# Expert loops of a macaron block: one buffer of gathered rows per tile, all gathers issued ahead of the scatters

## What is computed

```python
x = x + 0.5 * ffn(layernorm(x))     # mixture of 8 experts, top 1
x = x + mamba(layernorm(x))         # selective scan, 16 states
x = x + 0.5 * ffn(layernorm(x))     # same experts again

def ffn(x):
    route = softmax(x @ router_w + router_b)      # 8 experts
    max_prob, max_ind = max(route), argmax(route)
    for e in range(8):
        a, g = split(x @ w1[e])                   # 128 -> 2 x 512
        y = silu(a) * g @ w2[e]                   # 512 -> 128
        out = where(max_ind == e, y, out)
    return out * max_prob
```

## Time and profile before

| | |
|---|---|
| median of 3 runs | 427.21 us |
| span of the profiled execution | 449.5 us |
| TensorE matmul busy | 394.2 us, 88% |
| VectorE busy | 320.5 us, 71% |
| ScalarE busy | 264.8 us, 59% |
| GpSimd busy | 257.3 us, 57% |
| mean granted TensorE clock | 0.943 of full |

### The profile page before, as it was taken

How to read it: one execution, slowest core, us unless ns; L and a number is a source line. 1 busy time by engine, 2 the same in 40 slices (tenths; PEclk the granted TensorE clock), 3 DMA queues, 4 the chain that set the end, 5 groups by cost and what they waited for, 6 DMA issues and landing times. The chain is left out here.

```text
span 449.5 us, 8650 instructions
## 1 busy us (share of the span) xinstructions
PE 394.2 (88%) x3052; PEld 359.0 (80%) x3052; DVE 320.5 (71%) x497; ACT 264.8 (59%) x488; POOL 257.3 (57%) x186
## 2 busy tenths in 40 slices
PE   7978889994998899999998999998838886997894
PEld 7967889994763478899988899997838886997894
DVE  3664545552897999999999999999485853554452
ACT  3214333440597999999999999993443123342340
POOL 5045657543001049999999999998400063566633
PEclk9699999998799999999999999999965798999998
DMA  7828491111200484435344443441450311111200
GB/s 210 277 71 245 120 400 50 37 33 50 72 1 6 124 61 107 142 125 164 123 152 142 129 162 121 156 139 49 169 206 0 98 35 33 34 40 43 45 29 25
DMA packets 42731, 47.48 MB, mean 106 GB/s; under 512 B 13313, under 2 KB 34370, under 8 KB 42178
## 3 DMA queue, kind: packets, MB, share of 16 engines
q1 hardware_dynamic: 39746, 40.80, 30.1%
q0 software_dynamic: 2944, 6.13, 5.5%
HBM read 37.38 MB, written 9.54 MB: 104 GB/s over the span
## 5 line engine op out<-in xcount | busy, mean ns | idle before, releaser
L858 POOL TENSOR_TENSOR w_sb<-phase,w_sb 128x1024 f32<-128x1024 f32 x62 | 144.7, 2371 | 0.0
L939 DVE TENSOR_TENSOR_SCAN phase<-phase,psum 128x1024 f32<-128x1024 f32 x64 | 142.1, 2271 | 3.1 <-PE psum L1080 2.3
L648 PE MATMUL psum<-phase 128*128 128x128 f32 x736 | 91.4, 278 | 0.1
L376 POOL DMA_INDIRECT phase<-token_rows,token_row x46 | 46.9, 1020 | 76.4 <-DVE token_row L481 63.0
L648 PEld LDWEIGHTS psum<-phase 128*128 128x128 f32 x736 | 87.3, 194 | 0.4 <-issue 0.4
L996 ACT ACTIVATE phase<-dtxT,B_cols 128x256 f32<-128x256 f32 x192 | 80.2, 507 | 0.3
L1098 PE MATMUL psum<-ident,w_sb 128*128 128x128 f32 x512 | 67.8, 276 | 4.7 <-POOL w_sb L858 1.4
L1006 ACT ACTIVATE phase<-dt,neg_A 128x1024 f32<-128x1024 f32 x64 | 70.0, 1147 | 0.0
L1098 PEld LDWEIGHTS psum<-ident,w_sb 128*128 128x128 f32 x512 | 56.3, 141 | 10.6 <-POOL w_sb L858 8.9
L502 DVE TENSOR_TENSOR phase<-phase,psum 128x512 f32<-128x512 f32 x46 | 31.5, 685 | 45.9 <-PE psum L648 20.2
L563 ACT ACTIVATE phase<-psum 128x512 f32<-128x512 f32 x46 | 27.4, 595 | 60.2 <-PE psum L648 44.2
(11 more groups left out here) (171 smaller groups left out, 421.7 us busy)
## 6 DMA issues: line engine op xcount, KB each, us to landing
w_sb<-c_rows SPq DMA_DIRECT2D x32, 512.0 KB, 3.8
w_sb<-ffn_w SPq DMA_DIRECT2D x16, 512.0 KB, 7.2
B_diag<-dt SPq DMA_DIRECT2D x4, 1024.0 KB
phase<-B_diag SPq DMA_DIRECT2D x32, 128.0 KB, 3.7
token_rows<-x_tok SPq DMA_DIRECT2D x8, 264.0 KB, 4.4
w_sb<-ffn_w SPq DMA_DIRECT2D x8, 256.0 KB, 7.8
x_tok<-attn_x SPq DMA_DIRECT2D x4, 256.0 KB, 4.3
x_tok<-x_rows SPq DMA_DIRECT2D x4, 256.0 KB, 3.9
```

The source lines that it names most:

```text
L376: nc.gpsimd.indirect_dma_start(xs_sb[:, t % XS_RING, :], None, token_rows, bass.IndirectOffsetOnAxis(ap=token_row[:, t:t + 1], axis=0)).th ...
L648: last = nc.tensor.matmul(psum[:, 2 * k + part, c * P:(c + 1) * P], w1_tile[:, t % W1_RING, part * F + c * P:part * F + (c + 1) * P], xsT_ ...
L858: nc.gpsimd.tensor_tensor(hC[:, k % HC_RING, :], H[:, k % H_RING, :], C_sb[:, j % C_RING, :], ALU.mult).then_inc(M["hC_ready"], 1)
L939: nc.vector.tensor_tensor_scan(H[:, k % H_RING, :], dA[:, k % DECAY_RING, :], dBx_bank[k % SLOTS], 0.0, ALU.mult, ALU.add).then_inc(M["sca ...
```

## The change

A buffer of gathered rows for every tile (23 in place of 10). GpSimd issues all 23 gathers of a layer one behind the other and then all 23 scatters. The ten semaphores of the gathers stay, so gather t from 10 on now waits until gather t - 10 has landed, in place of waiting for give(t - 10). The ring of four results stays.

```diff
-    XS_RING, AHEAD, YS_RING = 10, 8, 4
+    XS_SEMS, YS_RING = 10, 4
...
-            (P, XS_RING, RW), (P, TURN_RING, D), (P, TURN_RING, P), (P, W1_RING, 2 * F), (P, 2, F), (P, U_RING, F),
+            (P, SLOT_TILES, RW), (P, TURN_RING, D), (P, TURN_RING, P), (P, W1_RING, 2 * F), (P, 2, F), (P, U_RING, F),
...
+        def await_rows(engine, f, t):
+            engine.wait_ge(f["xs_loaded"][t % XS_SEMS], f["xs_before"][t % XS_SEMS] + 16 * (t // XS_SEMS + 1))
+
         def ffn_gpsimd(pool, f, into):
 
             def gather(t):
                 if t == FULL:
                     pool.wait_ge(f["token_row_ready"], 2)
-                if t >= XS_RING:
-                    pool.wait_ge(f["ys_ready"], t - XS_RING + 1)
-                nc.gpsimd.indirect_dma_start(xs_sb[:, t % XS_RING, :], None, token_rows,
+                if t >= XS_SEMS:
+                    await_rows(pool, f, t - XS_SEMS)
+                nc.gpsimd.indirect_dma_start(xs_sb[:, t, :], None, token_rows,
...
-            for t in range(AHEAD):
+            for t in range(SLOT_TILES):
                 gather(t)
             for t in range(SLOT_TILES):
-                if t + AHEAD < SLOT_TILES:
-                    gather(t + AHEAD)
                 scatter(t)
```

More of the change, by code:

```diff
@@ L224, in ffn_sems @@
         def ffn_sems(tag, n):
-            xs_before = [16 * n * len(range(k, SLOT_TILES, XS_RING)) for k in range(XS_RING)]
+            xs_before = [16 * n * len(range(k, SLOT_TILES, XS_SEMS)) for k in range(XS_SEMS)]
             f = {n: sem(f"{tag}_{n}") for n in (
@@ L235, in ffn_sems @@
             return f
-        xs_loaded = [sem(f"xs_loaded{k}") for k in range(XS_RING)]
+        xs_loaded = [sem(f"xs_loaded{k}") for k in range(XS_SEMS)]
         ys_stored = [sem(f"ys_stored{k}") for k in range(YS_RING)]
@@ L373, in gather @@
                     pool.wait_ge(f["token_row_ready"], 2)
-                if t >= XS_RING:
-                    pool.wait_ge(f["ys_ready"], t - XS_RING + 1)
-                nc.gpsimd.indirect_dma_start(xs_sb[:, t % XS_RING, :], None, token_rows,
+                if t >= XS_SEMS:
+                    await_rows(pool, f, t - XS_SEMS)
+                nc.gpsimd.indirect_dma_start(xs_sb[:, t, :], None, token_rows,
                                              bass.IndirectOffsetOnAxis(ap=token_row[:, t:t + 1], axis=0)
-                                             ).then_inc(f["xs_loaded"][t % XS_RING], 16)
+                                             ).then_inc(f["xs_loaded"][t % XS_SEMS], 16)
             def scatter(t):
@@ L507, in give @@
                 dve.wait_ge(f["ys_psum"], t + 1)
-                dve.wait_ge(f["xs_loaded"][t % XS_RING], f["xs_before"][t % XS_RING] + 16 * (t // XS_RING + 1))
+                await_rows(dve, f, t)
                 if t >= YS_RING:
@@ L511, in give @@
                 nc.vector.scalar_tensor_tensor(out=ys_sb[:, t % YS_RING, :], in0=ys_bank(t),
-                                               scalar=xs_sb[:, t % XS_RING, PROB:PROB + 1],
-                                               in1=xs_sb[:, t % XS_RING, 0:D], op0=ALU.mult, op1=ALU.add
+                                               scalar=xs_sb[:, t, PROB:PROB + 1],
+                                               in1=xs_sb[:, t, 0:D], op0=ALU.mult, op1=ALU.add
                                                ).then_inc(f["ys_ready"], 1)
@@ L543, in norm @@
             def norm(t):
-                act.wait_ge(f["xs_loaded"][t % XS_RING], f["xs_before"][t % XS_RING] + 16 * (t // XS_RING + 1))
+                await_rows(act, f, t)
                 if t >= TURN_RING:
                     act.wait_ge(f["xsT_psum"], t - TURN_RING + 1)
-                xs = xs_sb[:, t % XS_RING, :]
+                xs = xs_sb[:, t, :]
                 nc.scalar.activation(xsn_sb[:, t % TURN_RING, :], xs[:, 0:D], ACT.Identity, bias=xs[:, SHIFT:SHIFT + 1],
```

## The result

The changed kernel took 447.47 us (median of 4 runs, 446.35 to 448.74), the kernel before, in the runs set beside it, 426.95 (426.31 to 433.03): a ratio of 1.0447, 95% interval 1.04 to 1.0494, slower by 20.5 us. The forecast was 444.4 with a range of 433 to 453.

What follows compares the result with a forecast made beforehand. TensorE was taken as the bound, at 2.79 us a tile. Stalls of 5.2 us (loop two) and 8.6 (loop one) plus 3.4 of clock made 17.2: 427.2 + 17.2 = 444.4 us, range 433 to 453.

Steps and rivals of the forecast that it cites:

- Late signals: Both expert loops before the change: late TensorE signals, 19.7 of 22.3 us between span and median, hardly in timed runs.
- Clearing the trace: Both expert loops: sums made as if no signals were late, at 2.79 us a tile from the start.
- When the first scatter goes: GpSimd, both loops: fifteen more gather steps of 1.27 us put scatter 0 at 58.3 and 392.0.
- The price of 451 us: Gathers beside VectorE's copies: about ten of fifteen steps lose up to 0.69 us each, time some 451 us.
- The landing: Scatter 0 lands 2.9 us after its start in a free queue, releasing give(4) at 394.9 in loop two.
- the slack: TensorE, both loops: 4.7 us of work left between give(4)'s delay and the stop at down(6).
- The big stores: Loop one: scatter 0 meets four 1 MB stores, lands at 65 (61.2 to 68), TensorE stands 8.6 us.
- The clock: Half clock behind each loop's TensorE stall: 1.7 us each, 3.4 together, bounds 0 and about 5.
- The free queue: Rival, loop one: scatter 0 lands in 2.9 us there too; 440.6 us, or 437.2 without clock loss; chance 0.24.
- The wait is not there: Rival, both loops: slack behind give(4) is 10 us, nothing stops, time stays at 427; chance 0.03.
- Everything longer: Rival: gather steps of 1.38, loop one landing at 68, 5 us of clock; 450.7 us; chance 0.11.
- The rival on the other side: Not slower: late signals are real, come with gathers; packing them gains 12 us, both loops; 421.6 us; chance 0.12.

Runs made afterwards that it cites:

- the pair of runs made for it: Changed kernel with delayed plain DMAs replacing gathers 9 to 22, without and with the 1 MB stores held back until scatter 3 landed: 452.94 and 448.0 us.
- the filler run: Changed kernel with delayed plain DMAs replacing gathers 9 to 22, plus identity matmuls on TensorE ahead of down(6): 454.7 us, ratio 1.0148.
- the delayed plain run: Changed kernel with plain DMAs replacing gathers from tile 9 on, a GpSimd memset behind each restoring the delay: 452.94 us, ratio 1.0148.

## Why the prediction was right

**Late signals.** "I take it that timed runs hardly have these late signals." For the comparison this holds: a profiled run of the changed kernel has none, and the difference of the medians is what the gaps sum to. As a general statement it is wrong: on chips 0, 13 and 15 the timed runs of before take 449.5 to 451.2 us, and the trace's span of 449.5 with 1.7 us added is 451.2. The trace on record and the times on record look like two different chips or conditions. By the forecast's own list ("I am wrong if timed runs carry the late signals") it fails on those chips: on chip 0 the change costs 22 us too, but by the hold-up beside the gathers and not by the ring. That the size is alike is chance. Clearing the trace was right for this comparison, but the reasons given for it couldn't tell a chip's habit from profiling.

**When the first scatter goes.** Forecast 30.1 and 30.0 us behind the first gather, measured 30.68 and 31.15. The gather steps that stand beside VectorE's pick are 0.3 us longer: 375.85 to 377.41 is 1.56, beside the copy of 375.60, and the undisturbed step is 1.25. Fifteen steps took 1.31 us each in loop one and 1.36 in loop two, where the forecast had 1.27. The forecast named the rule of the Trainium skill (SBUF — State Buffer, "SBUF: two separate sides") by which such a step would lose up to 0.69; the trace agrees in direction and gives less than half of that. It doesn't refute the rule, since the copy runs beside this gather for 0.44 us only. The later start is worth 0.5 us in loop one and 1.2 in loop two. The price of 451 us that the forecast put on the rule counts the lost steps of one loop; 6.9 us in loop two and the 11.6 us bound in loop one give some 454.

**The landing.** Forecast 2.9 us in a free queue, measured 2.40 in loop two. The stop there was forecast as 5.2 us and is 5.62, which is luck in part, since four errors nearly cancel: scatter 0 starts 1.2 us later, lands 0.5 faster, give(4)'s own time is 0.9 later (the first give stands at 374.85, 12.7 us behind the first gather, and the forecast had 11.8), and the slack is 0.7 shorter.

**The big stores.** The mis-sized term. Forecast landing 6.7 us behind its start, "a little past the middle"; measured 8.30, and 8.00 against 2.42 in the pair of runs made for it. The forecast's own upper bound (68, a stop of 11.6) would have been nearer. The loop's stop is 10.98 and not 8.6 us: 1.6 of the 2.4 us are the landing, 0.5 the later start and 0.4 the shorter slack, less 0.1 for give(4)'s own time. So the landing is the largest single part of the 3.1 us that the forecast fell short, and about half of it. The rule of the Trainium skill (DMA: Bandwidth & Descriptors, "Queues, rings and completion order") by which engines take turns packet by packet gave 440.6 us; the trace doesn't agree with what was drawn from it, that a small scatter gets through quickly.

**The slack.** Forecast 4.7 us between give(4) and TensorE's stop. Four tiles of 2.79 us behind this trace's first gives (39.3 and 374.8) the fifth was due at 50.5 and 386.0, so the delays are 15.3 and 9.7 and the slack 15.3 - 11.0 = 4.3 and 9.7 - 5.6 = 4.1. The forecast's slack was about half a microsecond too long.

**The clock.** Forecast 3.4 us, read from the changed kernel's rows 4.0. The level is shown (0.50 in the windows, full again by 70); the price is a reading, since in the filler run only the down block stood at full clock.

**The rivals.** The free queue fell with the landing in loop one. "The wait is not there" fell with TensorE's two stops: the slack is 4.1 to 4.3 us and not 10. "Everything longer" (450.7) lies about as far above the measured 447.5 as the forecast lies below. It was the nearer on the stores (11.6, measured 10.98) and on the steps of loop two (1.38, measured 1.36), and too high on the landing in loop two and on the clock (5, read 4.0). The rival on the other side deserves its chance of 0.12 in hindsight more than its text: on three chips its premise is true, the late signals are real and come with the gathers. Its conclusion is the reverse of what happens: packing the gathers makes them worse, 473 against 450. Only plain DMAs in place of the gathers, which fetch other rows, bring the time down, to 436.

**What stays open.** On the comparison's chip the ring wait was read and summed, not removed: the edits ran only where before takes some 450 us. The ring of eight should bring that chip back to about 427; this is argued and not shown. Why TensorE is held up beside indexed DMAs on some chips and not on that one, and by which path, no run here tells. That it is the indices is not shown either: the delayed plain run has nearly the pace of the gathers, but a plain DMA also reads one row 128 times over. No version was found that beats both kernels and computes the same.

## What to carry to other kernels

An issue order on one engine is also the order in which other engines' buffers come free: count the issue slots that stand ahead of the first release, multiply by the step, add the landing, and compare with ring size times the period of the bounding engine; here the release came 34 to 39 us behind the first gather and was wanted after 24. Where stores fill the DMA engines, take a landing as ending late in their time and not in its middle: here the share was full or nearly so from 56 to 66, and the landing came at 65.8. And when a trace's span is far from the median of the runs, the cause may be the chip; run the same kernel on another one before explaining either.

## What the runs showed of the hardware

- On chips 0, 13 and 15, while GpSimd issued indexed DMAs 1.25 us apart, TensorE got through a single matmul about every 2 us (chips 0 and 15), and VectorE stood up to 18 us for its results; the more in a row, the more was lost (450, 453.5 and 471 to 474 us for 8, 12 and 23). Plain DMAs by GpSimd didn't do it (436), nor did they at a pace of 1.37 us. In the comparison's trace the same program ran with TensorE fully busy.
- An indexed scatter beside four stores of 1 MB landed in 8.0 to 8.8 us in three runs, without them in 2.4.
- Issuing an indexed gather costs GpSimd 0.94 us and 0.30 before it, a plain DMA 0.54 to 0.59; beside a copy of VectorE the gather's step is 0.3 longer.
- Behind TensorE's stops of 11.0 and 5.6 us the granted clock was at half, and the down and hidden block there took 1.7 and 2.3 us longer.
- A run's time is its span and 1.7 to 1.9 us here.
